# A fused two-layer network on one core: new instruction orders, and six spare bf16 matmuls on PE ahead of the wait for the normalised output of the second attention

## The reference

```python
x = L0_attn_hidden_states                                   # 16 x 256 x 128
x = _layernorm(x + _L0_attn_ref(x, ...), axis=-1)           # softmax attention, 16 heads of 64
x = _layernorm(x + _L0_ffn_ref(x, ...), axis=-1)            # router, 64 tiles, spline, layer norm
x = _layernorm(x + _L1_attn_ref(x, ...), axis=-1)           # linear + windowed attention, gate
x = _layernorm(x + _L1_ffn_ref(x, ...), axis=-1)            # below
# _L1_ffn_ref: h = layernorm(x); q, k, v = h @ Wq, h @ Wk, h @ Wv  (16 heads of 64)
# q, k = l2norm(q) * q_scale, l2norm(k) * k_scale; causal softmax(10 q k^T) v; @ Wo
# h = layernorm(out); gate = softmax(h @ gate_w + gate_b)
# hid = gelu(h @ w1[e] + b1[e]); moe = sum_e gate[e] * (hid @ w2[e] + b2[e]); layernorm(moe)
```

## Time and profile before

| what | us |
|---|---|
| median of 3 runs | 2451.48 (2449.78 to 2452.81) |
| the profiled execution | 2448.45 |
| its span, first to last instruction | 2446.7 |
| PE busy | 2219.9 (91%) |
| DVE busy | 1570.6 (64%) |
| ACT busy | 1366.2 (56%) |
| POOL busy | 848.0 (35%) |
| mean granted clock of PE | 0.961 |

### The profile page before, as it was taken

The page is one execution under the profiler, slowest core; times in us unless marked ns, Lnnn a source line. Parts: engine busy times, 40 slices in busy tenths (PEclk is TensorE's granted clock), DMA queues, the critical chain, the costliest instruction groups (busy, mean ns, idle before and its releaser), DMA issues.

```text
span 2446.7 us, 43966 instructions
## 1 busy us (share of the span) xinstructions
PE 2219.9 (91%) x16096; PEld 1544.8 (63%) x16096; DVE 1570.6 (64%) x4247; ACT 1366.2 (56%) x3798; POOL 848.0 (35%) x1010
## 2 busy tenths in 40 slices
PE   7758998999989999999999999899998989999797
PEld 5545656756668566675666765676666756667465
DVE  4566676576656766667665767657676676666742
ACT  4436573755647655476555756465563764546442
POOL 2313461045510544106431256113561054510630
PEclk9878999999999999999999999999999999998899
DMA  4000000000010000110001000000001000010001
GB/s 145 27 1 1 1 10 27 18 31 1 10 35 10 31 10 1 44 31 2 10 1 44 32 1 10 18 27 31 1 10 33 13 31 1 1 35 10 31 1 48
DMA packets 24561, 50.43 MB, mean 21 GB/s; under 512 B 3285, under 2 KB 3869, under 8 KB 23965
## 3 DMA queue, kind: packets, MB, share of 16 engines
q1 hardware_dynamic: 24348, 47.62, 6.0%
HBM read 45.52 MB, written 2.10 MB: 19 GB/s over the span
## 4 chain that ended last, share of the span: by engine, by line
PE 71%; DVE 14%; POOL 6%; issue 5%; ACT 4%; DVEq 0%; ACTq 0%; POOLq 0%
PE ps L1439 9%; PE ps L1460 9%; PE ps L865 5%; PE ps L638 5%; PE ps L833 4%; PE ps L1396 4%; PE ps L655 4%; PE ps L1379 3%; PE ps L1472 3%; PE ps L593 3%; PE ps L1336 3%; PE ps L1347 3%; PE ps L747 3%; PE ps L764 2%; PE ps L800 2%
## 5 line engine op out<-in xcount | busy, mean ns | idle before, releaser
L1005 POOL TENSOR_TENSOR rstd<-ve,half_neg 128x4 f32<-128x4 f32 (+1 forms) x56 | 66.9, 1194 | 1016.1 <-DVE ve L986 1016.1
L1460 PEld LDWEIGHTS ps<-wbuf,QK 128*128 128x128 f32 x2048 | 265.4, 191 | 108.9 <-issue 101.6
L1259 POOL TENSOR_TENSOR E<-E,ri 128x512 f32<-128x512 f32 x240 | 248.3, 1041 | 192.8 <-DVE ri L1058 192.7
L1563 ACT ACTIVATE QK<-ps,cols 128x512 f32<-128x512 f32 x256 | 172.9, 686 | 219.0 <-PE ps L1439 218.6
L888 ACT ACTIVATE E<-ps,nm 128x256 f32<-128x256 f32 x480 | 224.7, 481 | 107.7 <-DVE nm L1051 106.8
L1439 PE MATMUL ps<-h2T,wbuf 128*128 128x512 f32 x512 | 277.9, 632 | 0.2
L1460 PE MATMUL ps<-wbuf,QK 128*128 128x128 f32 x2048 | 269.0, 275 | 0.2
L1689 POOL TENSOR_TENSOR work<-work,ri 128x128 f32<-128x128 f32 x480 | 231.4, 508 | 103.5 <-DVE ri L1612 103.3
L1682 POOL TENSOR_TENSOR rn<-ss,half_neg 128x8 f32<-128x8 f32 x120 | 195.7, 1638 | 168.7 <-DVE ss L1588 167.8
L1523 ACT ACTIVATE work<-ps,nm 128x128 f32<-128x128 f32 x480 | 198.9, 427 | 73.8 <-DVE nm L1603 72.6
L1051 DVE TENSOR_REDUCE nm<-ps 128x2 f32<-128x512 f32 x256 | 168.8, 684 | 65.2 <-PE ps L638 64.1
(11 more groups left out here) (279 smaller groups left out, 4537.3 us busy)
## 6 DMA issues: line engine op xcount, KB each, us to landing
wbuf<-in_w SPq DMA_DIRECT2D x128, 256.0 KB, 3.2
xT<-in_xT SPq DMA_DIRECT2D x8, 256.0 KB, 2.7
xr<-in_xr SPq DMA_DIRECT2D x8, 256.0 KB, 3.0
bias_t<-in_bias_t SPq DMA_DIRECT2D x1, 2048.0 KB
out_y<-xn SPq DMA_DIRECT2D x8, 256.0 KB, 2.1
wqkv<-in_wqkv SPq DMA_DIRECT2D x1, 1536.0 KB
wo<-in_wo SPq DMA_DIRECT2D x2, 512.0 KB, 8.8
rows<-in_rows SPq DMA_DIRECT2D x1, 531.0 KB, 7.1
```

The costliest lines, as they stand in the source:

```text
L1259: nc.gpsimd.tensor_tensor(L.E[:, g % 4, :, :], L.E[:, g % 4, :, :], L.ri[:, g, :].unsqueeze(2).broadcast_to((P, NT, S)), ALU.mult)\
L1460: last = nc.tensor.matmul(bank2[2 + x % 2][:, t * P:(t + 1) * P], hid[:, x % 2, c, t * P:(t + 1) * P], w2[:, x % WB, c, :], start=(c == 0) ...
```

## The change

Two edits of code and new strings for every engine:

1. `spare_work` issues six matmuls whose two operands are the bf16 identity, 512 columns each, into bank2[1]. Nothing reads the result. `second_pe` calls it between two yields, after the heads of the second attention and before the wait for `o2_ready`.
2. In the second attention's heads a `yield` splits the segment that adds the causal mask from the one that computes the scores, so that something can be put between them.
3. The strings of `ORDER` are new in all kinds of part; the last part's kind is renamed from "second" to "last".

```diff
+        def spare_work(pe, bank, n):
+
+            for _ in range(n):
+                nc.tensor.matmul(tri(bank, 4), ident_bf[:, :], ident_bf[:, :].unsqueeze(1).broadcast_to((P, 4, P)),
+                                 start=True, stop=True)
+
...
                                          causal[:, :].unsqueeze(1).broadcast_to((P, 2, P)),
                                          start=True, stop=False, skip_group_check=True)
+                yield
+                if u < HP:
                     for t, o in ((0, slice(0, P)), (1, slice(P, 3 * P))):
...
                 yield from second_heads_pe(pe, second_a, 0, 0)
             yield
+            spare_work(pe, bank2[1], 6)
+            yield
             pe.wait_ge(s["o2_ready"], upto("o2_ready", 1))
             transposed(bank2[2], xn2).then_inc(s["o2_tr"], 1)
...
     ("both", "gpsimd"):
-        "000111010111100001010111010101011001111111111111101001100101010101010101010110011010000000110",
+        "000111010111100001100110011110101010111111111111101010101010011100010101010101011001000000110",
...
-KINDS = ["first", "both", "both", "second"]
+KINDS = ["first", "both", "both", "last"]
```

More of the change, by code:

```diff
@@ L73 @@
-        "000000111110000001001101100001111111011101001000000000000000000000000000100000000000000000100010"
-        "000010001100000100000101011101010000000000111101011111011011000000000010",
+        "001000011111110111110111010001110101111111111110111100011111101110100000011111000000111110010110"
+        "110011111000000111110000000011111000000111110011111011111011111111101111111111011111111110111111"
+        "111001111110111001000100111100000101110100001011011001000111100010001111000010111001000001111100"
@@ L79 @@
-        "000000001001000000000022000002000202200222222",
+        "000011111111101100110101110111110110110101111100001100110011110011110010111101010111010011011110"
+        "000111001111101111110110101111111111000101111011011011011011000011111100011110000111010101110010"
+        "101110010101111010010011100101110001101110000111111001101010101111111111110111111111011111010011"
+        "110101010000000000000000000001000100000000020000022000202200222222",
     ("both", "scalar"):
-        "110000111111011010011111011000111111110000111100001111000011111111000011110000011110001111111111"
@@ L82 @@
[L82 to L83 removed]
+        "110010011111110010011111001100111111110000111100001111000011111111000011110000011110001111111111"
+        "111111011110011101111101111111100000111100001111000011110000111100001111000011110000111100000111"
+        "110001110100111111101111111111111110111010100111001110000000000000000000000000000000002222022222"
@@ L84 @@
         "222",
     ("both", "gpsimd"):
-        "000111010111100001010111010101011001111111111111101001100101010101010101010110011010000000110",
+        "000111010111100001100110011110101010111111111111101010101010011100010101010101011001000000110",
     ("both", "sync"):
[L88 to L91, removed]
+        "1111101111",
@@ L92 @@
+    ("last", "vector"):
+        "000000000000010000111111101001111100110111101001111011111111011110011000111100001110000000001101"
+        "111010000111100010011110000011101110000111010000111110000001111100010111100000111000110010000000"
         "00000000000000000000000000000000000",
-    ("second", "tensor"):
-        "000100000011001011111001100110111010111110110011001001111000001110001111001010010110100101011001"
-        "00011110010110100111001001111000001100100000000000000000000000000000000000000",
@@ L96 @@
[L96 to L100, removed]
+    ("last", "tensor"):
+        "001000000010011011111001100111100101011111110011001001111100000011110010011110000111010001011100"
+        "010111010100011011001001011101000111100100011111000000110010000000000000000000000000000000000000"
+        "00",
@@ L101 @@
+    ("last", "scalar"):
+        "000000000010111110011000111001111111111111000000001111000011110000111100001111000011110000111100"
+        "001111000011111000001110000000000000000000000000000000000000",
+    ("last", "gpsimd"):
+        "000011101101110011010100110010110001101010110100000",
 }
-KINDS = ["first", "both", "both", "second"]
+KINDS = ["first", "both", "both", "last"]
 def merged(order, *programs):
```

20 lines of the change are left out of this document (8 added, 12 removed).

## The result

The changed kernel takes 2406.57 us (median of 4 runs, 2405.76 to 2407.10), the kernel before beside it 2450.63 us (2449.18 to 2452.81). The ratio is 0.9819, with a 95% interval of 0.9802 to 0.9836: 1.8% faster. The forecast of 2423.0 had the sign and most of the mechanisms right, and the time lies near the low end of the range of 2405 to 2445. The gain is 44 us where 28.5 were forecast. The profiled execution lasts 2407.10 us with a span of 2405.3; its span is 41.4 us shorter than that of before.

A forecast was written before the change was run, and what follows sets the result against it. PE was taken as the bound, busy 2219.9 of 2446.7 us, so only its work, waits and clock count. Terms of 7.7 + 8.3 + 6.4 + 5.3 + 0.8 = 28.5 us less gave a median of 2423.0, range 2405 to 2445.

The forecast's parts named there:

- A: Start of parts 1 to 7: scores ahead of xn3's transposes fill 1.1 of a 1.80 us wait; -7.7 us.
- A2: Value matmuls at a part's start (L1336) keep full clock in five of six parts, 1.66 us each; -8.3 us.
- B: End of heads: POOL's L1277 moved earlier, so DVE's four L996 make xn2 ready 0.92 us sooner in seven parts; -6.4 us.
- B2: Behind the wait for xn2, a later or shorter clock fall gives 0.75 us in each of seven parts; -5.3 us.
- window stage: Its matmuls go two expert groups later; costed at nothing, with -0.5 to +1.6 us a part.
- prologue: Its new order was costed at nothing, with +-2 us.
- part 8: Spare matmuls covered by its 4.28 us wait for xn2, clock may fall later; -0.8 us, from 0 to -1.7.
- The doubt on BN_STATS: DVE's work on acc might be held until POOL's L1277 ends: up to +0.8 us a part; taken as 0.
- The spares: Six matmuls ahead of L680, 1.3 us, lying in PE's waits: cost on the path 0, at most +0.5 us a part.
- The rest: Mask split, window-stage matmuls, router's copies and prologue order only move work between waits and full places; costed at nothing.
- rival 3: Slower: second sequence's early heads lose the clock, +4.4 us a part, +30.5 in seven, giving 2467.9 us; chance 0.09.

The follow-up runs named there:

- scores alone: Kernel before with one PE step moved: in parts 1 to 7 the first four score matmuls stand ahead of xn3's transposes; 2428.67 us, ratio 0.9924.
- the two experiments on the scores: Kernel before with scores ahead of xn3's transposes: 2428.67 us; changed kernel without spare matmuls, scores behind those transposes again: 2413.77 us.
- xb alone ahead: Kernel before with only POOL's xb moved ahead of the inverse square root for xn2 in parts 1 to 7: 2444.09 us, ratio 0.9995.

## Why the prediction was right, and where it was short

The terms, over the 41.4 us of the two spans. The sizes are from the traces.

| term | forecast | measured | from |
|---|---|---|---|
| A, scores into the wait | -7.7 | -7.8 | 1.80 to 0.69 us, seven parts |
| A2, clock at the start | -8.3 | -7.7 | sum of the value matmuls' time above 3.70 us before |
| B, xn2 earlier | -6.4 | -8.4 | 3.26 to 2.06 us of waits |
| B2, clock at the end of the heads | -5.3 | -3.5 | scores alone: a part 2.71 shorter on average, less A and A2 |
| heads | 0 | -11.8 | (0.86 + 0.82) x 7 |
| window stage | 0 | -2.9 | 0.42 x 7 |
| prologue | 0 | -1.6 | first value matmul at 219.89, before at 221.44 |
| part 8 | -0.8 | +3.1 | 175.44 against 172.39 |

They add to -40.6; 0.8 us is not placed. The terms from the heads on are part 4's times seven, and part 7 gained more: from the kernel with the scores alone to the changed one without spares it became 5.2 us shorter, part 4 3.3. The prologue's term is no larger than its scatter, since its first value matmul starts at 220.3 to 223.4 us in the five traces with the old strings and at 218.4 to 220.4 in the nine with the new ones.

**A and A2** were right in place and reason: the wait left for ACT's copies is the 0.69 us that was put at 0.7, and the two experiments on the scores show that their place removes the fall. A's size was right too; A2's is so partly by luck. It was five parts at 1.66 us, and it was six at 1.28 on average: part 4, from which the price was read, has the dearest start of the seven. **B** had its mechanism right. Its size was the upper end of its bounds, 1.2 us, because the wait of DVE for wo2 goes as forecast, and the step that failed is the choice of 0.92 over 1.2 though all the rows for 1.2 were there. The doubt on BN_STATS came out at 0: 0.87 us beside xb. The Trainium skill ("SBUF — State Buffer", section "Who interferes with whom") says that a DVE instruction with at most one SBUF input outside the two-port modes doesn't contend with GpSimd; this trace now agrees for BN_STATS, and shows the copy of acc out of PSUM at its usual 0.42 us with xb starting within it.

**The spares** cost nothing that was measured, as forecast, though they take 1.46 us and not 1.3. The step that failed is the link to B2. It was expected that less idle ahead of the wait delays the fall, and B2's -5.3 us were put down to the spares and the shorter wait together. The half-clock time did go from 10.2 to 6.8 us, but it does so without the spares, and with the scores alone, where the wait is still 1.98 us. In the changed kernel the six spares of the title bring nothing that these runs can tell; in the kernel before they bring 2.3 us, at the edge of what the interval can tell.

**Heads** are the step that was missing. "The rest" was costed at nothing because PE's work is the same. But the sum should have gone over the waits of the heads, each 0.2 to 0.9 us and there in every part: an order that lets two thirds of a microsecond less idle through, twice a part, and shortens the recorded busy time a little is 11.8 us. Which of the moves in the heads does it stays open. The upper bounds for that (PE's 18.5 us of waits a part) were in view. **Part 8** was forecast with the wrong sign, since only its long wait was looked at and not its early heads, whose rows the change reorders too, nor the clock with which it starts; rival 3 named that mechanism for parts 1 to 7 only, where PE held 1.00.

The forecast median misses by 16.4 us. 3.5 of them are the step from span to median: the profiled execution of before lay 3.03 below its median, that of the changed kernel 0.5 above. The other 12.9 are heads 11.8, window stage 2.9, B 2.0, the prologue 1.6 and A 0.1, less 3.9 for part 8 and 2.4 for the clock, with the 0.8 not placed. That the time still lies within the range is luck: the range reached down to 2405 because a clock that stays high at the end of the heads was given 18 us (with part 8), and of that came 3.5; what fills the place are the waits of the heads, which had no term.

## What to carry to other kernels

Sum the small waits of PE over a repeated part before costing "moved" work at nothing: here 1.7 us a part, 1.3 of it idle time, were the largest term. A wait can cost more than its length when the clock falls behind it, and shortening it halfway may bring nothing (xb alone ahead: a ratio of 0.9995); take it away, and time several runs. Spare matmuls in a wait can hold the clock through it and still bring nothing, when the fall then comes further on: look first at what stands there, and at what PE would wait for if it came earlier. And a stretch whose own order is untouched can change its time through the clock that it is handed, so try each part's order beside the orders it will run with.

## What the runs showed that was not expected

- The same order shows different half-clock stretches from part to part and from run to run, and the length depends on where the fall begins: 17.1 us where it begins 0.36 to 0.75 us ahead of the gate's 8-column matmuls, 6.8 us where it begins between 0.2 us ahead and 2.2 us behind their start, 13.7 us in the two parts where it begins 2.4 to 2.6 us behind. With xb alone ahead the runs of one kernel spread by 25 us (mean granted clock 0.965 at 2438.6 us, 0.953 at 2463.7), while the changed kernel's runs lie within 1.4. What decides where the fall begins stays open; the 1.06 us wait goes with the long stretches in 9 of 28 parts, and no run here changed that wait in small steps.
- Holding the clock at full through the gate's, the router's and the experts' first matmuls brought the next matmuls forward by 0.6 to 1.8 us, and the fall that came behind them took it back in six of seven parts (part 5, without it: 1.1 us shorter).
- With the same order, part 8 takes 175.4 to 175.5 us in three kernels and 172.1 to 172.8 in three others, by whether the clock falls in its early heads.
